# Attention and mixture-of-experts block on one core: the row swap of the rotary embedding done by a VectorE shuffle out of PSUM, and the early x units in other stages

## What is computed

```python
q = split_heads(x @ Wq); k = split_heads(x @ Wk); v = split_heads(x @ Wv)   # 16 heads of 64
x1, x2 = (x[..., 0::2], x[..., 1::2])                    # rotary embedding, on q and k
rot = jnp.stack([x1 * cos - x2 * sin, x1 * sin + x2 * cos], axis=-1)
attn = softmax(where(causal, q @ k.T * scale, -inf)); out = (attn @ v) @ Wo + bo
# ffn: gate softmax over tokens, top 8 tokens for each of 32 experts, merged; two layers with gelu; scattered back
```

## Time and profile before

| what | value |
|---|---|
| median of 3 runs | 1391.26 us |
| the profiled execution | 1394.52 us, its span 1392.7 us |
| granted TensorE clock, mean | 0.984 |
| PE, DVE, ACT, POOL busy | 1326.8, 876.9, 640.9, 976.6 us |
| DMA | 188.88 MB, mean 136 GB/s |
| transfers t_raw to t_swap | 248 of 128.0 KB, median 2.1 us to landing |

### The profile page before, as it was taken

One profiled execution on the slowest core, in us unless ns is written; L12 is line 12 of the kernel. 1 busy time (PEld: TensorE's weight loads), 2 busy tenths in 40 slices (PEclk: granted clock), 3 DMA queues, 4 the chain that ended last, 5 costly groups with the idle time before them and its releaser, 6 DMA issues.

```text
span 1392.7 us, 31589 instructions
## 1 busy us (share of the span) xinstructions
PE 1326.8 (95%) x11676; PEld 870.7 (63%) x11676; DVE 876.9 (63%) x1185; ACT 640.9 (46%) x969; POOL 976.6 (70%) x661
## 2 busy tenths in 40 slices
PE   6898999999899999999899999999999999999998
PEld 5565666655565555556667676666656776666656
DVE  5687667865555666556555666665757666665753
ACT  3445655543453344435433434544444434455542
POOL 2676667865665666558666777887879777888954
PEclk9898999999999999999999999999999999999999
DMA  5322333487678667774552221212232121222111
GB/s 179 116 73 86 140 138 123 169 287 249 221 257 298 217 219 240 270 245 154 150 167 77 89 85 62 78 63 78 92 108 89 63 77 62 77 66 81 61 58 62
DMA packets 122753, 188.88 MB, mean 136 GB/s; under 512 B 29616, under 2 KB 57808, under 8 KB 122608
## 3 DMA queue, kind: packets, MB, share of 16 engines
q1 hardware_dynamic: 92176, 112.51, 24.6%
q10 hardware_dynamic: 30384, 74.23, 15.5%
q0 software_dynamic: 48, 0.13, 0.1%
HBM read 130.71 MB, written 22.54 MB: 110 GB/s over the span
## 4 chain that ended last, share of the span: by engine, by line
PE 71%; DMA 10%; DVE 7%; POOL 3%; issue 3%; ACT 3%; SPq 2%; ACTq 0%; DVEq 0%; POOLq 0%
PE t_pO L1550 15%; PE t_pF L1525 11%; PE t_pA L1448 8%; PE t_pB L1448 6%; PE t_pF L1508 5%; DMA t_swap<-t_raw 4%; PE t_pA L1472 3%; PE t_pC L1472 3%; DMA r_s<-t_rcomp 2%; PE t_pC L1599 2%; PE t_pB L1599 2%; PE t_pA L1453 2%; PE t_pC L1559 2%; PE t_pB L1453 2%; POOL t_acc L762 2%
## 5 line engine op out<-in xcount | busy, mean ns | idle before, releaser
L762 POOL TENSOR_TENSOR t_acc<-t_acc,t_PT 128x1024 f32<-128x1024 f32 (+3 forms) x256 | 433.2, 1692 | 153.9 <-ACT t_PT L839 133.4
L737 POOL TENSOR_TENSOR t_swap<-t_swap,t_sin 128x512 f32<-128x512 f32 x124 | 169.9, 1370 | 199.8 <-DMA t_swap<-t_raw 198.3
L1550 PE MATMUL t_pO<-t_PT,t_V 128*64 128x512 f32 (+3 forms) x1536 | 292.0, 501 | 0.1
L839 ACT ACTIVATE t_PT<-t_pA 128x1024 f32<-128x1024 f32 x192 | 169.6, 883 | 260.0 <-PE t_pA L1460 226.0
L1525 PE MATMUL t_pF<-t_xT,t_wqk 128*128 128x512 f32 x756 | 215.1, 421 | 6.7 <-issue 3.9
L740 POOL TENSOR_TENSOR t_rot<-t_rot,t_swap 128x512 f32<-128x512 f32 x124 | 184.1, 1485 | 9.7
L1550 PEld LDWEIGHTS t_pO<-t_PT,t_V 128*64 128x64 f32 x1536 | 93.7, 137 | 139.8 <-issue 123.3
L861 ACT ACTIVATE t_raw<-t_pF 128x512 f32<-128x512 f32 x124 | 74.0, 597 | 195.5 <-PE t_pF L1525 135.3
L1525 PEld LDWEIGHTS t_pF<-t_xT,t_wqk 128*128 128x128 f32 x756 | 136.0, 193 | 43.8 <-issue 15.6
L1122 DVE TENSOR_TENSOR t_LO<-t_rot,t_HI 128x512 fp32r<-128x512 f32 x124 | 147.9, 1193 | 7.1 <-ACT t_HI L871 7.1
L839 ACT ACTIVATE t_PT<-t_pB 128x768 f32<-128x768 f32 (+1 forms) x192 | 141.9, 739 | 13.6 <-PE t_pB L1460 7.6
(11 more groups left out here) (233 smaller groups left out, 2414.3 us busy)
## 6 DMA issues: line engine op xcount, KB each, us to landing
t_w1t<-in_L_ffn_w ACTq DMA_DIRECT2D x32, 1024.0 KB, 6.2
t_w2t<-in_L_ffn_w ACTq DMA_DIRECT2D x32, 1024.0 KB, 9.0
t_swap<-t_raw SPq DMA_DIRECT2D x248, 128.0 KB, 2.1
t_OT<-r_s SPq DMA_DIRECT2D x128, 128.0 KB, 3.0
t_wqk<-wqk_s SPq DMA_DIRECT2D x24, 512.0 KB, 3.7
xt_s<-t_xs SPq DMA_DIRECT2D x6, 1024.0 KB, 5.0
t_xT<-xt_s ACTq DMA_DIRECT2D x6, 1024.0 KB, 6.2
t_wvs<-wv_s SPq DMA_DIRECT2D x12, 512.0 KB, 5.0
```

Of the source, the lines that this page charges most:

```text
L737: pool.tensor_tensor(swap_of(r), swap_of(r), sin[:, c * BANK:(c + 1) * BANK], ALU.mult).then_inc(sin_sem, 1)
L762: pool.tensor_tensor(a[:, :, off:], a[:, :, off:], pt, ALU.add).then_inc(acc_done, 1)
L839: act.activation(PT[:, n % PTS, :, 0:w], bank[:, :, 0:w], ACT.Exp, scale=SCALE).then_inc(exp_done, 1)
L1550: mm = pe.matmul(pO[h * DH:(h + 1) * DH, off:], v, PT[:, n % PTS, h, 0:w], start=(j == 0), stop=(j == 4 * c + 3))
```

## The change

The exchange of rows is done by one VectorE instruction, `stream_shuffle` with the list i ^ 1, that reads pF and writes t_swap. It stands in `rope` ahead of the multiplication by cos. ScalarE's copy to t_raw, SyncE's two transfers for each fill, the buffer t_raw and the semaphores that go with them are gone. The x units and normalisations stand in other stages: x units in (1, 4), (1, 5), (2, 3), (2, 4), (3, 3), (3, 4) in place of (1, 5), (2, 1), (2, 3), (3, 1), (3, 3), (4, 1). Statistics, variance, root and moments stand one stage earlier each.

```diff
-UNITS_AT = {(0, 5): ("logit", 0), (1, 5): ("x", 1, 0), (2, 1): ("x", 1, 1), (2, 2): ("logit", 1), (2, 3): ("x", 2, 0),
-            (3, 1): ("x", 2, 1), (3, 2): ("logit", 2), (3, 3): ("x", 3, 0), (4, 1): ("x", 3, 1), (4, 2): ("logit", 3),
+UNITS_AT = {(0, 5): ("logit", 0), (1, 4): ("x", 1, 0), (1, 5): ("x", 1, 1), (2, 2): ("logit", 1), (2, 3): ("x", 2, 0),
+            (2, 4): ("x", 2, 1), (3, 2): ("logit", 2), (3, 3): ("x", 3, 0), (3, 4): ("x", 3, 1), (4, 2): ("logit", 3),
...
-STATISTICS_AT = {(0, 2): [(1, 0)], (0, 3): [(1, 1)], (0, 4): [(2, 0)], (0, 5): [(2, 1)], (1, 0): [(3, 0)], (1, 1): [(3, 1)]}
+STATISTICS_AT = {(0, 1): [(1, 0)], (0, 2): [(1, 1)], (0, 3): [(2, 0)], (0, 4): [(2, 1)], (0, 5): [(3, 0)], (1, 0): [(3, 1)]}
...
@@ @block.sync
-                    sp.wait_ge(raw_done, r + 1)
-                    if r >= EARLY + 2:
-                        sp.wait_ge(sin_done, r - EARLY - 1)
-                    for o in range(2):
-                        sp.dma_start(swap[o::2, r % 2, :], raw[1 - o::2, :]).then_inc(swapped[r % 2], 16)
@@ @block.gpsimd
-                swap_ready(pool, r)
+                pool.wait_ge(swapped, r + 1)
@@ @block.scalar
-                    r = ROPE[f]
-                    if r > EARLY:
-                        swap_ready(act, r - 1)
-                    act.activation(raw_of(r), bank, ACT.Copy).then_inc(raw_done, 1)
...
-                if (P, g) == (1, 3):
+                if (P, g) == (1, 2):
                     root(2)
@@ @block.vector
-                dve.wait_ge(raw_done, r + 1)
+                dve.wait_ge(proj_done, FILL[f] + 1)
                 if r >= EARLY + 2:
                     dve.wait_ge(lo_done, r - 1)
+                dve.stream_shuffle(swap_of(r), fill_bank(f), [i ^ 1 for i in range(32)]).then_inc(swapped, 1)
                 dve.tensor_tensor(rot_of(r), fill_bank(f), cos[:, c * BANK:(c + 1) * BANK], ALU.mult).then_inc(cos_done, 1)
...
+                if (P, g) == (1, 1):
+                    variance(2)
                 if (P, g) == (1, 2):
-                    variance(2)
-                if (P, g) == (1, 3):
                     moments(2)
```

More of the change, by code:

```diff
@@ L268, in attend_block @@
         wraw = sb("t_wraw", [P128, KT, 2 * P128])
-        raw = sb("t_raw", [P128, BANK])
         swap = sb("t_swap", [P128, 2, BANK])
@@ L335, in attend_block @@
         fill_read = sem("t_fill_read")
-        raw_done = sem("t_raw_done")
-        swapped = [sem(f"t_swapped{i}") for i in range(2)]
+        swapped = sem("t_swapped")
         cos_done = sem("t_cos_done")
@@ L372, in attend_block @@
         first_loaded = [sem(f"t_first_loaded{n}") for n in range(3)]
-        first_swapped = [sem(f"t_first_swapped{r}") for r in range(EARLY)]
         first_turned = [sem(f"t_first_turned{r}") for r in range(EARLY)]
@@ L645, in _ @@
                     first_output()
-                f = fill_of(P, g)
-                if f in ROPE:
-                    r = ROPE[f]
-                    sp.wait_ge(raw_done, r + 1)
-                    if r >= EARLY + 2:
-                        sp.wait_ge(sin_done, r - EARLY - 1)
-                    for o in range(2):
-                        sp.dma_start(swap[o::2, r % 2, :], raw[1 - o::2, :]).then_inc(swapped[r % 2], 16)
                 n2 = normalise_of(*STAGES[s - 2]) if s >= 2 else None
@@ L828, in exp @@
                 if n < PTS:
[L829 to L833, removed]
+                    for r in range(2 * (n % 2), 2 * (n % 2) + 2) if n >= 2 else ():
+                        act.wait_ge(first_turned[r], 1)
                 else:
@@ L841, in evict @@
             def evict(f):
[L843 to L849, removed]
-                            act.wait_ge(pv_done, chunk_index(2 * unit - 3, 1, 3) + 1)
-                        dst = V0[:, unit % 2, t:t + 2, :]
-                    else:
-                        if unit >= 1:
-                            act.wait_ge(pv_done, chunk_index(2 * unit - 1, 1, 7) + 1)
-                        dst = V1[:, t - 4:t - 2, :]
-                    act.activation(dst, bank.rearrange("p (t n) -> p t n", t=2), ACT.Copy).then_inc(fill_read, 1)
-                else:
-                    r = ROPE[f]
-                    if r > EARLY:
-                        swap_ready(act, r - 1)
-                    act.activation(raw_of(r), bank, ACT.Copy).then_inc(raw_done, 1)
+                act.wait_ge(proj_done, FILL[f] + 1)
+                unit, t = f[1:]
+                if t < 4:
+                    if unit >= 2:
+                        act.wait_ge(pv_done, chunk_index(2 * unit - 3, 1, 3) + 1)
+                    dst = V0[:, unit % 2, t:t + 2, :]
+                else:
+                    if unit >= 1:
+                        act.wait_ge(pv_done, chunk_index(2 * unit - 1, 1, 7) + 1)
+                    dst = V1[:, t - 4:t - 2, :]
+                act.activation(dst, fill_bank(f).rearrange("p (t n) -> p t n", t=2), ACT.Copy).then_inc(fill_read, 1)
             def high(f):
@@ L1043, in _ @@
                     high(f)
-                if fill_of(P, g):
+                if fill_of(P, g) and fill_of(P, g)[0] == "v":
                     evict(fill_of(P, g))
@@ L1295, in first_sine @@
                 c = f[2]
-                swap_ready(dve, r)
+                dve.wait_ge(swapped, r + 1)
                 dve.tensor_tensor(swap_of(r), swap_of(r), sin[:, c * BANK:(c + 1) * BANK], ALU.mult).then_inc(first_sin[r], 1)
```

23 lines of the change are left out of this document (3 added, 20 removed).

## The result

The changed kernel's median is 1385.5 us (1379.37 to 1391.22, 20 runs), against 1390.25 us for the kernel before (1382.17 to 1394.5, 20 runs). The ratio is 0.9966, with a 95% interval of 0.9951 to 0.9981: 4.75 us faster, a quarter of the 19.8 us that were forecast. The time lies just inside the upper end of the range (1361 to 1386), where rival A had placed it (1385).

The account below looks back on a forecast made before the run. TensorE's own work was taken as the bound, 1326.8 of 1392.7 us. The terms 6.5 + 5.0 + 4.5 + 3.5 - 4.0 + 1.8 + 2.5 = 19.8 us off 1391.3 gave 1371.5 us, range 1361 to 1386.

Parts of the forecast that it names:

- rival A: Half the gain comes back elsewhere as other traffic is the limit and VectorE's work costs its upper bound: 1385 us, chance 0.20.
- (a): Expert stages: without the copy's wait for transfers the slot is read sooner, five of six TensorE waits go: 6.5 us.
- (c): Behind each GELU: without the copy exp comes sooner, 4.0 us, and v fills wait less, 0.5 us: 4.5 us.
- (d): Clock: fills and smaller matmuls after the stalls of (a) and (b) no longer run at 1.2 GHz: 3.5 us.
- Part 2: The shuffle's cost on VectorE: 77 us more work, mostly covered, net -4.0 us, bounds 0 and -10.
- (b): At 675 us: ScalarE's copy waited for transfers, exp came late; TensorE's 5.05 us wait goes: 5.0 us.
- The shuffle's length: On VectorE: 0.69 us for one shuffle, taking 0.60 us of VectorE's time.
- The late pairs: At g = 0, 0.44 us of room against 0.60: 3.5 us lost over some 22 pairs without experts, 1.5 us taken.
- The start and pairs 0 to 5: Four early shuffles ahead of the first scores, and pairs where VectorE is fullest: 2.5 us lost.
- +1.8 for the x units: Units leaving g = 1 save 4.8 us; VectorE's added work in (P, 4) costs 1.0 us in three stages.
- +2.5 for moments and variance: Statistics moved a stage earlier: a third of 7.7 us of wait and slow clock at (1, 3), bounds -3 and 7.7.
- Rival B: Slower: a shuffle of 1.2 us makes g = 0, g = 1 and early pairs lose time: about 1401 us, chance 0.07.

Follow-up runs that it names:

- experiment 8: Kernel before, transfers kept, with two t_raw buffers from pair 8 on: 1377.16 us, ratio 0.9923.
- experiment 5: Changed kernel with a third t_rot buffer and t_LO behind everything else of the stage on VectorE in g = 0 and 1, pairs 6 to 13: 1365.85 us.
- experiment 7: Changed kernel, third t_rot buffer, t_LO last in pairs 6 to 13, shuffle and cos ahead of t_LO in pairs 14 to 30 (g = 0, 1): 1366.33 us.
- experiment 11: Changed kernel with the x units alone back in their stages of before: 1393.58 us, ratio 1.0017 against the kernel before.
- experiment 10: Changed kernel with every shuffle done twice, once into a spare buffer: 1438.92 us, ratio 1.0353 against the kernel before.

## Why the prediction missed

**(a), (c) and their share of (d), 12.75 us in the expert stages: right as a size, and not what the change gained.** Removing the copy's wait by a second buffer won 12.6 us there (experiment 8). The shuffle won 2.8. The step that failed is in Part 2, where the shuffle was priced at nothing in the expert pairs ("the shuffle takes the copy's place"), and the loss counted in "some 22 pairs without experts" alone. In an expert pair VectorE pays 0.64 us for the shuffle and 0.67 us for a t_OT that now starts in the middle of GpSimd's sin, both ahead of the slot's read, and in g = 1 the shuffle stands behind a t_LO that waits for t_HI behind the GELU. With t_LO out of the way and a third t_rot buffer (experiment 5) a pair takes 43.58 in place of 44.73 us, 9.2 us in eight, of which the buffer has 2.8: 2.8 + 9.2 gives back 12.0 of the 12.75. That is a sum; the whole stretch took 8.7 us less than before in the profile of experiment 5 and 15.6 less in that of experiment 7, with 5.4 and 0.9 us of waits for t_wqk in the two runs.

**(b), 5.0 us and its share of (d), 1.75: right in place, too small.** The stretch won 9.2 us, since the 2.70 us wait at 719 us, which I had left as one that stays, went with the other.

**The shuffle's length, 0.60 us of time: right** (0.64 from start to start, and 740 ns for one where 690 was said). The estimate from the Trainium skill (VectorE: DVE Perf Modes, "The perf-mode tier table") was 0.60 us; the time from start to start is 7% above it, the instruction itself 23%. The 124 shuffles took 725 to 766 ns, whatever GpSimd did. That agrees with the rule cited from the Trainium skill (GPSIMD Engine Reference, "8. Key points"), which holds for two SBUF inputs and two-port modes. The row that the prediction set beside this rule, t_mean, has one SBUF tile as its input, so it can speak for the second of the two conditions at most. What I left out were the neighbours: t_OT and t_LO have two SBUF inputs and met GpSimd at new times.

**The late pairs, "0.16 us lost in each of some 22 pairs", 1.5 us taken: mis-sized.** The step that failed is "the tightest such place in a pair is g = 0". g = 0 paid 0.25 us, near the 0.16. But g = 1, which I never looked at, paid 0.42: its room was 1.19 us, and shuffle and stretched t_LO took 1.55. The shuffle alone would have fitted. Together 0.67 us in a pair, 6.8 us in the last stretch. The hope that GpSimd's new phase would help was wrong in sign: t_LO is the longer for it. About half of the 0.67 us goes with a third t_rot buffer (experiment 5).

**The start and pairs 0 to 5.** Forecast: -2.5 for shuffles, +1.8 for the x units, +2.5 for moments and variance, +1.8 together. Measured -0.9 + 4.5 - 2.8 = +0.8. The units are worth 7 us beside a shuffle (experiment 11), the statistics nothing that a run tells; the new 1.0 us waits in the stage after (P, 4) have the size that was forecast, but they are for ScalarE's exp and stand at 0.99 us in the run without a shuffle too, so VectorE is not their cause. Not foreseen was the loss from (4, 5) to (6, 1), where the first expert slot is read: 2.27 us of wait in place of 1.25 and 1.13 us (1.36 with the stages alone, so it is the shuffle's). In this stretch two executions of the same code also differ by 3.1 us (60.41 and 57.31).

**The sum.** The bounds for the shuffle, 0 to -10, were too narrow. The late stretch (6.8), the expert pairs (9.2) and the stretch to (6, 1) (2.8) cost 18.8 us, against 4.0 taken: 14.8 us too little. The two profiles of each kernel stand 6.6 us apart in the mean, 13.2 less than 19.8; (b) gave 2.4 of the 14.8 back, and the other terms together took 0.8. Rival A named the right time, but that was luck: its mechanism was traffic, and of that only a late t_wqk shows (2.3 and 4.6 us of waits in the two profiles of after, 1.0 and 2.1 in those of before); it was right in that VectorE's work would cost its upper bound and more. Rival B's sign would have needed 0.95 us for one shuffle; by experiment 10 another 0.64 us costs 54 us, so the change stood nearer to that than its own length says.

## What to carry to other kernels

When an operation moves from an idle engine to one that another engine waits for, price it in every stage, and look for the smallest room in each, not in the one stage that looks fullest; where it takes the place of a wait, ask whether that wait is the last to end. Removing a delay also moves the engine behind it: ask what then runs beside what. A second profile of the kernel before tells which waits are steady: here the 3.56 us at 116 us, with 7.7 us at stake, came again as 1.71 us with no low clock behind it. Here the order of VectorE's queue and one more buffer were worth more than the change: with t_LO behind the reads and a third t_rot, 1366 us in place of 1385.5. When an experiment needs a second edit to be possible, as the buffer here, give that edit a run of its own.

## What the runs showed of the hardware

- Each shuffle is two instructions in the trace, a load of the mask (13 ns) and the shuffle of 128 x 512 float32 out of PSUM (740 ns); from the start of the load to the start of the next instruction they cost 0.65 us on average.
- A VectorE multiplication with two SBUF inputs of 128 x 512 (t_OT) took 0.68 us when it started as a GpSimd multiplication of the same size ended, and 1.42 us when it started 0.40 us into one of 1.28 us, which is 0.88 us to its end and 0.54 more. In the first case GpSimd's next operation took 1.72 us in place of 1.28. A shuffle out of PSUM took 725 to 766 ns in all 124 cases.
- An instruction of VectorE that waited for the semaphore of the one directly in front of it started 1.93 us after the start of that one (1.80 us long); without that wait it started 1.75 us after the start of one that took 1.82 us, before its end.
- A wait of 2.27 us was followed by a fill at the 1.2 GHz level in one execution (2.93 us, first row) and by one at 2.4 GHz in another of the same kernel (1.65 us, second row):

```profile
289.13 2.93 PE L1482 MATMUL t_pF<-t_xT,t_wqk 128*128 128x512 f32 x6
```

```profile
286.60 1.65 PE L1482 MATMUL t_pF<-t_xT,t_wqk 128*128 128x512 f32 x6
```
